# Layer 0's projection and turn back moved away from layer 1's query and key projections, and a one-hot turned as one tile

## The reference

```
h = layernorm(x) * (1 + ca) + sa
x = x + ga * attention(h)
h = layernorm(x) * (1 + cb) + sb
x = x + gb * ffn(h)
```

```
sel = argmax(gates, axis=-1)
gm = one_hot(sel, EXPERTS) * gates
values = einsum('bhne,ehdk,bnd->bhnk', gm, value_experts, x)
attn = softmax(where(causal_mask, min, q @ k))
out = einsum('bhne,ehkd,bhnk->bhnd', gm, output_experts, attn @ values)
```

## Time and profile before

| what | value |
|---|---|
| median of three runs | 758.41 us (758.11 to 759.46) |
| span of the profiled execution | 758.0 us |
| TensorE (PE) busy | 738.9 us, 97% |
| VectorE (DVE) busy | 550.8 us, 73% |
| ScalarE (ACT) busy | 383.1 us, 51% |
| POOL busy | 187.3 us, 25% |
| mean granted clock of TensorE | 0.997 of full speed |

### The profile page before, as it was taken

The page is one execution under the profiler, slowest core; times in us unless marked ns, Lnnn a source line. Parts: engine busy times, 40 slices in busy tenths (PEclk is TensorE's granted clock), DMA queues, the critical chain, the costliest instruction groups (busy, mean ns, idle before and its releaser), DMA issues.

```text
span 758.0 us, 16817 instructions
## 1 busy us (share of the span) xinstructions
PE 738.9 (97%) x6559; PEld 558.0 (74%) x6559; DVE 550.8 (73%) x1642; ACT 383.1 (51%) x1063; POOL 187.3 (25%) x235
## 2 busy tenths in 40 slices
PE   7899999999999999999999999999999899999996
PEld 5666757775786578657865776688578778999996
DVE  4877785868867886778677867787959664255997
ACT  3755656355545654564456445643561446554422
POOL 0232522154015402530253025304210422000000
PEclk9999999999999999999999999999999999999999
DMA  7950020402040204020302130113204304000000
GB/s 229 397 120 1 29 57 2 112 1 57 8 106 2 57 19 96 2 56 20 96 2 55 28 87 18 41 39 76 57 2 113 112 3 111 1 1 1 16 21 22
DMA packets 55702, 43.07 MB, mean 57 GB/s; under 512 B 37900, under 2 KB 48804, under 8 KB 54216
## 3 DMA queue, kind: packets, MB, share of 16 engines
q1 hardware_dynamic: 55624, 42.01, 20.7%
HBM read 32.42 MB, written 9.58 MB: 55 GB/s over the span
## 4 chain that ended last, share of the span: by engine, by line
PE 85%; DVE 9%; ACT 2%; DMA 1%; issue 1%; POOL 1%; SPq 0%; DVEq 0%; ACTq 0%
PE ps L1755 15%; PE ps L1838 14%; PE ps L1898 8%; PE ps L2061 4%; PE ps L2039 4%; PE ps L1741 4%; PE ps L2008 4%; PE ps L1763 4%; PE ps L1850 3%; PE ps L1789 3%; PE ps L1776 3%; DVE shared L1484 2%; DVE shared L1477 2%; PE ps L1705 2%; PE ps L1921 2%; PE ps L1933 2%
## 5 line engine op out<-in xcount | busy, mean ns | idle before, releaser
L1755 PE MATMUL ps<-veF,hB 128*128 128x512 f32 x256 | 121.5, 606 | 0.0
L1303 DVE COPY_PREDICATED shared<-ghot,ps 128x512 f32<-128x512 int32 x128 | 88.2, 726 | 3.4 <-PE ps L1755 0.6
L850 ACT ACTIVATE sc<-sc,nmax 128x128 f32<-128x128 f32 (+1 forms) x128 | 57.2, 447 | 58.3 <-DVE nmax L1289 58.3
L1755 PEld LDWEIGHTS ps<-veF,hB 128*128 128x128 f32 x256 | 45.2, 189 | 49.4 <-issue 40.5
L650 POOL TENSOR_TENSOR sc<-sc,rg 128x384 f32<-128x384 f32 x64 | 51.6, 827 | 70.0 <-DVE rg L1276 70.0
L707 POOL TENSOR_TENSOR ve<-mv,eps 128x2 f32<-128x2 f32 x24 | 8.6, 357 | 229.9 <-DVE mv L1189 229.9
L1838 PE MATMUL ps<-early_masks,oeF 128*128 128x256 f32 x256 | 62.9, 385 | 0.0
L1838 PE MATMUL ps<-wide,oeF 128*128 128x256 f32 x256 | 62.3, 386 | 0.0
L1898 PE MATMUL ps<-hC,early 128*64 128x128 f32 x1024 | 61.7, 275 | 0.1
L2039 PE MATMUL ps<-hE,veF 128*128 128x256 f32 x256 | 59.5, 382 | 0.3 <-ACT wide L959 0.3
L1898 PEld LDWEIGHTS ps<-hC,early 128*64 128x64 f32 x1024 | 55.6, 137 | 5.3 <-issue 3.4
(11 more groups left out here) (253 smaller groups left out, 1529.5 us busy)
## 6 DMA issues: line engine op xcount, KB each, us to landing
chosen<-hot_scratch SPq DMA_DIRECT2D x16, 512.0 KB, 5.8
v_scratch<-shared SPq DMA_DIRECT2D x16, 512.0 KB, 5.2
vg<-v_scratch SPq DMA_DIRECT2D x16, 512.0 KB, 5.4
veF<-in_L_ffn_value_experts SPq DMA_DIRECT2D x1, 2048.0 KB, 9.3
oeF<-in_L_ffn_output_experts SPq DMA_DIRECT2D x1, 2048.0 KB, 14.2
early<-in_L_attn_w_qkv SPq DMA_DIRECT2D x1, 1536.0 KB, 14.9
shared<-bias_scratch SPq DMA_DIRECT2D x2, 512.0 KB, 5.8
veF<-in_L_ffn_W SPq DMA_DIRECT2D x1, 1024.0 KB, 5.2
```

What stands on the lines that cost most here:

```text
L850: act.activation(v, v, ACT.Exp, bias=nmax[:, h % RING, t:t + 1], scale=-1.0, accum_out=denB[:, h * T + t:h * T + t + 1]).then_inc(s_("f_e" ...
L1303: dve.copy_predicated(val[:, t, :].rearrange("p (h k) -> p h k", h=HF), ghot[:, t * HF:(t + 1) * HF, e].bitcast(I32).unsqueeze(2) .broadca ...
L1755: pe.matmul(ps[:, vbank(j), :], tok(hB, t), veF[:, :].rearrange("p (h e k) -> p e h k", h=HF, e=EF)[:, e, :, :], start=True, stop=True).th ...
```

## The change

It has two parts. The one-hot of a batch, 128 tokens by (2 tiles x 64 choices), is turned by one transpose of 128 x 128 instead of two of 128 x 64; `hotT` holds the two tiles one below the other, and SP writes the scratch by two transfers.

The steps of layer 0's attention leave the query and key projections. PROJECT goes to the new place "turned" in `back1`, between the last turn of the weights and the product with the values; in the first round, which has no `back1`, it goes to the start of `front1`. ADD goes from "qk5" to "qk7", NORM from "qk7" to "v"; MODULATE stays at "s". New waits go with it: PROJECT waits for `f_ots`, the copy of the outputs out of bank 0, and the second half of the product with the values waits until ScalarE has copied `yT` out of bank 0 (`a_ys`).

```diff
-        hotT = sb("hotT", [HF * EF, N], U8)
+        hotT = sb("hotT", [T * HF * EF, P], U8)
...
-            in_front = {"qk3": (PROJECT,), "qk5": (ADD,), "qk7": (NORM,), "s": (MODULATE,)}
+            in_back = {"turned": (PROJECT,)}
+            in_front_first = {"start": (PROJECT,)}
+            in_front = {"qk7": (ADD,), "v": (NORM,), "s": (MODULATE,)}
...
-                if not first:
-                    back1(b - 1, alone, k)
                 more = [(masks, b + 1, 0, in_front_masks)]
+                if first:
+                    more.append((after_attn0, b + 2, k + 1, in_front_first))
+                else:
+                    back1(b - 1, beside((after_attn0, b + 2, k + 1, in_back)), k)
...
-                sp.dma_start(hot_dram, hotT[:, :]).then_inc(s_("hot_out"), 16)
-                sp.wait_ge(s_("hot_out"), b * 16 + 16)
+                for t in range(T):
+                    sp.dma_start(hot_dram[:, t * P:(t + 1) * P],
+                                 hotT[t * HF * EF:(t + 1) * HF * EF, :]).then_inc(s_("hot_out"), 16)
+                sp.wait_ge(s_("hot_out"), b * 32 + 32)
...
-                        act.activation(hotT[:, :], ps[0:HF * EF, 7, 0:N], ACT.Copy).then_inc(s_("f_hTs"), 1)
+                        act.activation(hotT[:, :], ps[:, 7, 0:P], ACT.Copy).then_inc(s_("f_hTs"), 1)
...
                     turned1(b, 2)
+                    beside("turned")
...
-                    if b > AHEAD:
-                        pe.wait_ge(s_("c_oca"), (b - AHEAD) * 8)
+                    if b > AHEAD + 1:
+                        pe.wait_ge(s_("c_oca"), (b - AHEAD - 1) * 8)
+                    if b >= AHEAD:
+                        pe.wait_ge(s_("f_ots"), b * 2)
...
-                        for t in range(T):
-                            mm = pe.transpose(ps[0:HF * EF, 7, t * P:(t + 1) * P],
-                                              ghot[:, t * HF:(t + 1) * HF, :].rearrange("p h e -> p (h e)"),
-                                              ident[:, :])
-                        mm.then_inc(s_("f_hT"), 1)
+                        pe.transpose(ps[:, 7, 0:P], ghot[:, :, :].rearrange("p h e -> p (h e)"),
+                                     ident[:, :]).then_inc(s_("f_hT"), 1)
...
-            def back1_paired(b, k):
+            def back1_paired(b, beside, k):
                 turn1(b, 2)
+                beside("turned")
                 pe.wait_ge(s_("f_o3"), b + 2)
...
                         pe.wait_ge(s_("n_h"), k + 1 + B)
+                        pe.wait_ge(s_("a_ys"), min(b + 4, B))
```

More of the change, by code:

```diff
@@ L1976, in back1 @@
                 if paired(b):
-                    back1_paired(b, k)
+                    back1_paired(b, beside, k)
                     return
```

## The result

The changed kernel takes **763.45 us** (762.88 to 764.60) where the kernel before takes 758.47 us (756.77 to 759.49): 5.0 us more, a ratio of 1.0063 with a 95% interval of 1.0051 to 1.0075. It is slower by 0.6%, as forecast (761.2 us, range 757.8 to 764.8), but by more than the +2.8 us of the sum: the time lies inside the range and just above the likely part of it, 759.3 to 763.3 us. The profiled execution took 763.29 us, with a span of 761.5 us.

The account below looks back on a forecast made before the run. TensorE's steps were taken to bound the kernel. Rounds 2 to 6 at +0.48 us each (+2.4), the first at +1.3 and the one-hot at -0.9 gave +2.8 us on 758.41: 761.2 us, range 757.8 to 764.8.

Parts of the forecast that it names:

- the sum: All terms added over six rounds and the one-hot: +2.8 us, from +0.8 to +6.4 us.
- What bounds the kernel: Inside the six rounds TensorE never stands still, so the time is the sum of its steps.
- Part 1: Projection and turn back leave the query and key projections, saving two shape changes to whole array and back: 0.67 us a round.
- Rival D: Shape-change time only moves to the steps' new places, leaving only the waits: 764.9 us; chance 0.05.
- Part 2: One one-hot transpose instead of two saves 0.11 us in each of eight batches, 0.9 us in all.
- Rival C: The one-hot's 128x64 shape costs a 0.36 us excursion per batch, now saved: 758.3 us, no change; chance 0.06.
- Part 3: The projection at its new place waits for VectorE's copy out of bank 0: 0.1 us a round.
- The first round's 0.6 us: With no transposes between, the first round's projection stands 0.6 us, once, for the copy out of bank 0.
- rival E: ScalarE's copy of yT is late for the product with the values' second half: 763.6 us; chance 0.07.
- Part 4: TensorE waits for xn behind the value projections, as masks and evacuations precede it on VectorE: 1.05 us a round.
- Rival B: VectorE is not late with xn, so the change gives what it saves: 755.0 us, faster; chance 0.16.

Follow-up runs that it names:

- x6: The changed kernel with two of the five early masks made behind all four evacuations of the values instead of ahead of them; 757.61 us.
- x8: The kernel before with one excursion more a round and no more work: the second tile's turn back goes behind part 6 of the projections; 760.51 us.
- x1: The kernel before with only the one-hot turned as one whole tile; 758.07 us, ratio 0.9993.
- x10: The changed kernel without the projection's already fulfilled wait on the emptied banks (c_oca); one execution for its trace, 764.07 us.
- x4: The kernel before with the one-hot as one tile and only the projection moved, turn back and normed tile left in place; 758.04 us.
- x5: The kernel before with the one-hot as one tile and only the turn back and normed tile moved, the projection left in place; 762.40 us.
- x3: The changed kernel with the transposes of xn moved from behind the value projections to the start of the products; 758.00 us.
- x9: The changed kernel with xn's transposes at the products, normed tile behind all evacuations, first round's projection back behind part 3, and the c_oca count left out; 755.40 us.

## Why the prediction was right in sign and short in size

- **What bounds the kernel**: right in the main. Every term that held or stopped TensorE came out in the time. That TensorE never stands still inside the rounds was not quite so: it pauses before the change too, by 1.30 and 0.75 us in the two executions.
- **Part 1, two excursions, -0.67 us a round**: right. One piece of 7.15 us instead of 7.44, a turn back and value projections of 3.71 us without the wait (x6) instead of 3.91, and a projection whose change of shape falls away: 0.29 + 0.20 + 0.19 us, the last by estimate, since the projection waits in its new place in every run. x8 measured one excursion at 0.30 us. Rival D, that the time only moves to the new places, is out by the same figures.
- **Part 2, the one-hot, -0.9 us**: within the measurement of x1 (-0.6 us, from -1.3 to +0.3). Rival C, 3.7 us less with the one-hot alone, is out.
- **Part 3, the wait for oT, +0.1 us a round**: the step that failed in size. The turn of the weights and the projection take 0.79 + 1.03 = 1.82 us in rounds 3 to 6, where 0.50 + 0.95 = 1.45 us would be free of waits, by estimate (four transposes; four records at 0.22 us and one change of shape): 0.37 us. Of these, 0.15 us are the fulfilled wait ahead of it, which the sum had at nothing (x10), 0.14 us the copy and its signal, and 0.08 us a slower first matmul behind the pause (0.29 us to the next start, the second and third record 0.22). Over five rounds this is 1.2 us more than the sum had, so the move of the projection gains nothing (x4). The first round's 0.6 us was right: L1798's steps took 1.43 us instead of 0.83.
- yT was in time: L1973 takes 2.15 us as before, so rival E is out. That its 763.6 us lie so near the measured 763.45 is chance.
- **Part 4, the wait for xn, +1.05 us in six rounds**: right to 0.01 us, as x5, x6 and x3 show from three sides. Rival B, no wait at all, would have needed the order of x6.
- **The sum**: by steps the change costs 1.14 us in the first round, 0.59 in the second and 0.74 in each of the next four, less 0.8 for the one-hot: 3.9 us against the predicted 2.8. The rest to 5.0 us is about what the unexplained pauses add; the sum had no term for them. That they belong to the change is likely from x5, x6 and x10, but only argued, and their cause stays open.

## What to carry to other kernels

Where one engine has no idle time, price a moved step by the start-to-start distances around it, and then walk the queue of the engine that feeds the next consumer: the move here saved its 0.67 us and lost 1.05 because two masks and two evacuations came to stand ahead of the operand. If a step is moved later, move its consumer later too, into work that needs no change of shape, and look for the second consumer of the same queue (x3, then x9). A count that is already fulfilled is not always free on a queue with no slack (0.15 us here, behind a wait that came late); where an earlier wait implies it, leave it out. And before two spans are compared, compare the granted clock by stretches: 1.3 us of the first pair lay there, and not in the change.

## What the runs showed of the hardware

The same addition on POOL (128 x 2) took 0.55 us in the changed kernel and 0.20 us in x6. POOL in the third round, changed kernel:

```profile
281.44 0.55 POOL L713 TENSOR_TENSOR ve<-mv,eps 128x2 f32<-128x2 f32 x1 [15.49 <-DVE mv L1196]
282.06 1.03 POOL L715 TENSOR_TENSOR rstd<-ve,half 128x2 f32<-128x2 f32 x1
```

and in x6:

```profile
279.37 0.20 POOL L713 TENSOR_TENSOR ve<-mv,eps 128x2 f32<-128x2 f32 x1 [15.48 <-DVE mv L1196]
279.64 0.70 POOL L715 TENSOR_TENSOR rstd<-ve,half 128x2 f32<-128x2 f32 x1
```

In the first, VectorE runs a mask from 281.27 to 281.93, and POOL's addition ends at 281.99; the second instruction lasts through the end of the next mask. In x6 VectorE reads accumulators at that time. It is the same in all rounds of the kernel before, the changed kernel, x4, x5, x6 and x9: the addition takes 0.55 us wherever a mask overlaps it and 0.19 or 0.20 us elsewhere.

That is why the wait in x6 went altogether. The expectation let xn start 1.58 us behind the sums, as before the change, where the addition stood behind a mask. In x6 xn starts 1.24 us behind them (279.20 to 280.44): 0.34 us less, about the 0.35 us that the addition no longer loses, and more than the 0.25 us that were to be left.

The Trainium skill says in SBUF — State Buffer, Summary: rules for kernel authors, that when a VectorE operation has two inputs from SBUF while a GpSimd operation (here POOL) reads SBUF, the second one to issue blocks until the first finishes. These rows agree for the addition, which ends 0.06 us behind the mask; how much of the second instruction was blocked they do not tell.
